# A selective scan after windowed attention on one core: TensorE's products dealt out anew over a chunk's slots, and one convolution tap moved to VectorE

## The reference, cut to what matters

```python
dt = softplus(einsum('nlr,dr->nld', dt, dt_proj_w) + dt_proj_b)
dA = exp(dt[..., None] * A)
dBx = dt[..., None] * Bm[:, :, None, :] * xc[..., None]
def step(h, inp):
    a, b, c = inp
    h = a * h + b
    return (h, jnp.sum(h * c[:, None, :], axis=-1))
```

## Time and profile before

| what | value |
|---|---|
| median of three runs | 10573.59 us (10556.45 to 10581.08) |
| the profiled execution's own time | 10566.67 us |
| its span in the trace | 10564.6 us |
| outside the span | 2.1 us |
| granted clock of PE, mean over the span | 0.899 |
| busy: PE, DVE, ACT, POOL | 8593.4, 8682.6, 6501.9, 6485.6 us |
| stage 1 ends, stage 2's first scan, its last scan ends | about 4.2 ms, 4228.1 us, 10266.8 us |

### The profile page before, as it was taken

One profiled execution on the slowest core, in us unless ns is written; L12 is line 12 of the kernel. 1 busy time (PEld: TensorE's weight loads), 2 busy tenths in 40 slices (PEclk: granted clock), 3 DMA queues, 4 the chain that ended last, 5 costly groups with the idle time before them and its releaser, 6 DMA issues. The chain is left out here.

```text
span 10564.6 us, 200712 instructions
## 1 busy us (share of the span) xinstructions
PE 8593.4 (81%) x61658; PEld 3655.3 (35%) x61658; DVE 8682.6 (82%) x10568; ACT 6501.9 (62%) x12597; POOL 6485.6 (61%) x4046
## 2 busy tenths in 40 slices
PE   6999999999899998877887877788887777787870
PEld 3555555555555554222222222222222222222220
DVE  6777777777777775999989999998989999998985
ACT  5666666666666665666656666665666666666653
POOL 3222222222222221888888898988888888888980
PEclk9999999999999998888888898988888889888885
DMA  2222322222322322111111111111111111111119
GB/s 68 69 69 70 77 71 69 69 69 71 80 74 73 75 74 52 33 41 33 37 37 33 36 39 33 41 33 33 40 35 33 41 33 36 39 33 35 40 40 277
DMA packets 855792, 591.01 MB, mean 56 GB/s; under 512 B 621424, under 2 KB 725872, under 8 KB 848464
## 3 DMA queue, kind: packets, MB, share of 16 engines
q1 hardware_dynamic: 751440, 423.61, 17.3%
q0 software_dynamic: 49152, 100.76, 2.6%
q10 hardware_dynamic: 54016, 51.91, 1.6%
HBM read 109.27 MB, written 103.81 MB: 20 GB/s over the span
## 5 line engine op out<-in xcount | busy, mean ns | idle before, releaser
L1217 POOL TENSOR_TENSOR b_hh<-b_hh,b_cn 128x1024 f32<-128x1024 f32 x1600 | 3833.7, 2414 | 496.0 <-DVE b_hh L1516 495.6
L1516 DVE TENSOR_TENSOR_SCAN b_hh<-b_dA,b_ub 128x512 f32<-128x512 f32 x2800 | 3369.6, 1206 | 0.0
L278 POOL DMA_DIRECT2D kvsel<-kv x1536 | 1103.1, 721 | 2885.3 <-issue 2455.3
L1357 ACT ACTIVATE b_dA<-b_db,b_negA 128x448 f32<-128x448 f32 x2800 | 1719.3, 633 | 1289.3 <-PE b_db L1609 1280.8
L1501 DVE TENSOR_TENSOR b_ub<-b_ub,b_bn 128x512 f32<-128x512 f32 x2800 | 1904.5, 680 | 543.2 <-PE b_ub L1609 528.0
L1609 PE MATMUL b_ub<-b_rows,b_pick 96*64 96x512 bf16 x6400 | 1407.6, 441 | 946.3 <-DVE b_hh L1516 901.3
L1609 PE MATMUL b_db<-b_rows,b_pick 96*64 96x512 bf16 x6400 | 1283.8, 424 | 203.5 <-ACT b_dA L1357 199.8
L1609 PEld LDWEIGHTS b_ub<-b_rows,b_pick 96*64 96x64 bf16 x6400 | 361.3, 110 | 3130.9 <-DVE b_hh L1516 2668.6
L554 DVE SCALAR_TENSOR_TENSOR oacc<-vpad,vec,oacc 128x1064 f32<-128x1064 f32 (+1 forms) x934 | 1199.7, 1302 | 11.4
L1645 PE MATMUL b_acc<-b_hh,b_gather 64*32 64x512 f32 x12800 | 1008.5, 692 | 3.0 <-POOL b_hh L1217 3.0
L395 ACT ACTIVATE prob<-score,nmax 128x256 f32<-128x256 f32 (+1 forms) x1600 | 735.9, 478 | 167.3 <-issue 96.1
(11 more groups left out here) (190 smaller groups left out, 13559.5 us busy)
## 6 DMA issues: line engine op xcount, KB each, us to landing
b_rows<-b_term SPq DMA_DIRECT2D x2400, 64.0 KB, 2.0
kvsel<-kv SPq DMA_DIRECT2D x1600, 64.0 KB, 2.1
kvsel<-kv POOLq DMA_DIRECT2D x1536, 64.0 KB
xpad<-in_x SPq DMA_DIRECT2D x18, 1568.0 KB, 10.7
ys<-ysb ACTq DMA_DIRECT2D x16, 1600.0 KB, 9.4
b_yc<-ys SPq DMA_DIRECT2D x100, 256.0 KB, 2.7
xr<-b_xo SPq DMA_DIRECT2D x100, 256.0 KB, 2.7
x<-x3pad SPq DMA_DIRECT2D x16, 1568.0 KB, 18.2
```

The costliest lines, as they stand in the source:

```text
L278: eng.dma_start(kvsel[:, slot, j, :, WPIX * t:WPIX * (t + 1)].unsqueeze(1), kv[:, bass.ds(at[t], 1), :, :]).then_inc((s_kv, s_kg)[j][slot] ...
L1217: nc.gpsimd.tensor_tensor(out=now, in0=now, in1=cn[:, par, :].unsqueeze(1).broadcast_to([C, 2, HT]), op=ALU.mult).then_inc(s_pm, 1)
L1357: nc.scalar.activation(later(dA[:, k % DEEP, :]), later(db[k % 2][:, :]), ACT.Exp, scale=negA[:, 8 * q + e:8 * q + e + 1]).then_inc(s_a, 1)
L1516: nc.vector.tensor_tensor_scan(hh[:, k // 2 % PDEEP, HT * (k % 2):HT * (k % 2 + 1)], rate, new, 0.0, ALU.mult, ALU.add).then_inc(s_sc, 1)
```

## The change

Three things are edited.

1. `PTAP` is 4: PE does four lepe taps and DVE 21, so `LEPES` is 63, and 38 instead of 35 of them are spread over the pairs.
2. PE's long products from slot 16 on stand elsewhere: `project_bc` in slots 17 and 21 (was 16 and 17), the second and third product of `conv_even` in slots 28 and 30 (was 26 and 28). Slots with repeats only are now 14, 16, 18, 20, 22, 26 and 29: no two of them are neighbours.
3. ACT's two `kept` follow: behind decay 24 and decay 28 (was 23 and 24).

```diff
-        PTAP = 5
+        PTAP = 4
...
                 decay(n, 23)
+                decay(n, 24)
                 if more:
                     kept(n + 1, nxt, 0)
-                decay(n, 24)
-                if more:
-                    kept(n + 1, nxt, 1)
                 decay(n, 25)
...
                 for k in range(28, 32):
                     decay(n, k)
+                    if k == 28 and more:
+                        kept(n + 1, nxt, 1)
...
-                    if s == 16 and more:
+                    if s == 17 and more:
...
-                    if s == 17 and more:
+                    if s == 21 and more:
                         project_bc(n + 1, nxt, 1, s_bn, ONE + 2 * n + 3)
...
-                    if s in (25, 26, 28) and before_end(n, 2):
-                        conv_even(n + 2, (25, 26, 28).index(s))
+                    if s in (25, 28, 30) and before_end(n, 2):
+                        conv_even(n + 2, (25, 28, 30).index(s))
```

## The result

The changed kernel takes 10401.73 us (median of four runs, 10394.62 to 10411.63), the kernel before beside it 10568.08 us. The ratio is 0.9843, 95% interval 0.9826 to 0.986: faster by 1.6%, about 166 us. The forecast of 10104 us promised 4.4%, and the range ended at 10270 us. The sign was right, the size was not.

What follows compares the result with a forecast made beforehand. Stage 2 was taken as bound by DVE's scans, lengthened by PE at low clock: 54.9 + 0.6 + 0.3 = 55.8 us a chunk against 60.4, so 460 us, plus 10 for the tap, giving 10104 us; range 10010 to 10270.

Steps and rivals of the forecast that it cites:

- What bounds the kernel: Stage 2: a chain through DVE's scans, lengthened by PE, late by 5.2 us a chunk where the clock is down.
- The fall behind slot 22 goes away: Units 20 to 31: project_bc in slot 21 keeps the clock up, worth 2.2 to 5.8 us a chunk.
- The rule that was weighed: TensorE clock: drops need long idle gaps, so order would not matter; the trace's fall followed pauses of about 1.1 us.
- POOL doesn't become the bound, but it has nothing left: Stage 2: POOL busy 53.6 us, under 54.9; slot 31's add waits for product 11, costing 0.6 us, bounds 0 and 1.2.
- Rival C: Chunk's end, slots 28 to 31: the fall moves there, all chunks take 65.5 us, 11074 us in all; chance 5%.
- Up to 4.8 us more where it ran over into the next chunk: Units 0 to 19: low clock carried over from slot 22's fall, 41.6 against 36.8 us, goes away too.
- The third term: Slots 6 and 8: the clock can still fall, 1.25 us in one chunk of four, so 0.3 us a chunk.
- The tap: Attention: moving one tap from PE to DVE gives -3.4 and +2.7 us an image, -10 us in all.
- No one engine is the bound: Attention, 107.2 us an image: PE busy 98.2, ACT 97.4, DVE 92.0, so the tap could give -110 to +62 us.
- The other signs: Profile after: clock 0.95 or more, L1501 idle about 90 us, units 20 to 31 in 18.1 to 19 us.
- Rival A: Slots 24 to 30 or behind 14 to 18: one fall left in every chunk, 57.1 us each, 10234 us; chance 15%.
- Rival B: Stage 2: the clock doesn't depend on the order, only slot 26's lost product helps, 10473 us; chance 6%.

Runs made afterwards that it cites:

- bc_alone: The kernel before with only project_bc in slots 17 and 21 and ACT's copies behind decays 24 and 28; 10483.8 us, ratio 0.9957.
- order_alone: The changed kernel with PTAP = 5 again, so only the long products and ACT's two copies move; 10440.54 us, ratio 0.9899.
- mid_early: The changed kernel with ACT's middle(0) of the next chunk moved in front of evac and decay 21; 10225.67 us, ratio 0.9697.
- tap_dropped: The kernel before with four taps on PE, the same twenty on DVE and tap 24 left out altogether; 10406.37 us, ratio 0.9871.
- tap_alone: The kernel before with PTAP = 4 and nothing else; 10441.34 us, ratio 0.9892.
- pool_less: The changed kernel with POOL's products of pairs 8 and 9 made for one unit instead of two; 10160.88 us, ratio 0.963.
- mid_on_before: The kernel before with only ACT's middle(0) moved before evac and decay 21; 10536.51 us, ratio 1.0002.

## Why the prediction was wrong, step by step

**What bounds the kernel: right.** The chain runs through DVE's scans, and PE's repeats and the clock lengthen it. **The fall behind slot 22 goes away: right,** in all chunks; the add of slot 23 takes 1.09 us, and bc_alone shows that the `project_bc` in slot 21 does it. **The rule that was weighed** was one of the Trainium skill ("TensorE: Matmul & The Clock Gate", section "Why this matters for your kernels"), which ties drops to long idle gaps; by it the order would not have mattered. The runs disagree: the kernel before, bc_alone and order_alone have the same work on PE and their falls at other places, and the fall in the timeline above followed pauses of 0.58 and 0.94 us. Only the falls at a loop's end have a long pause beside them (2 to 3 us), and in the changed kernel 18 of those 31 begin ahead of it.

**"POOL doesn't become the bound, but it has nothing left": this step failed.** It compared POOL's busy time, 53.6 us, with the chunk's 54.9, and priced the one wait it saw, at the add, at 0.6 us. What counts is where in the chunk POOL's idle time lies. Nearly all of it is in front of product 4 and of `last`; behind them stands an unbroken row of 22.8 us (6748.03 to 6770.81) that begins with a wait for ACT, and this row's end holds up scan 30 and the adds of slots 27 and 31. Measured, a chunk at full clock is 56.2 us instead of 55.5, small in itself. But with the pauses that it makes in PE the clock falls in 41 chunks more, and mid_early, which takes this wait away, gains 187 us of stage 2, 1.9 us a chunk (154 us by the ratios, 1.5 a chunk). The forecast had taken 0.6 for it, with 1.2 as the upper bound.

**Rival C's mechanism was real, in 41 of 98 chunks,** and had only 5% because it was priced as all or nothing. Its price was too high: the chunk of 59.0 us above lost 2.8 us against one at full clock, not 9.7, and the mean loss is 2.0. With that price the point from which it turns the sign would never be reached. A mechanism of this kind belongs into the forecast as a term, not aside as a rival.

**"Up to 4.8 us more where it ran over into the next chunk": this reading failed.** I took the 41.6 us of the third chunk for the effect of the fall at slot 22. It is the loop's end, which came with its own fall all 31 times, before as after. The clue was there: three cuts, and one of them a pass's last chunk. The loss was a part of the 60.4 us and no part of what the change mends, but the forecast took all of 60.4 - 54.9 for lateness that goes away. It had no term for the loop's end, and it costs 1.6 to 1.7 us a chunk. The third term, one fall in four chunks at scans 5 to 9 with 1.25 us each, came out right as a product: 37 of 98 chunks had one, with about 0.9 us each, so 0.3 us a chunk.

The sum, then: 55.8 us forecast, less the 0.6 that it held for POOL, plus 1.9 for POOL's row and the falls behind it and 1.6 for the loop's end, gives 58.7, where 59.2 was measured. The rest is what even mid_early's best chunks have over the floor of 54.9 (55.4 us in the mean of those without a fall). Of the 3.4 us that were missed, the loop's end is the largest part.

**The tap: the sign was right, the term mis-sized.** -10 us was -3.4 from PE and +2.7 from DVE an image. Measured, in the same units: PE 72 / 16 = -4.5, DVE +1.6, so -2.9 us an image. "No one engine is the bound" held. I halved PE's relief, and two thirds of it came through; and I charged DVE the difference between a pair with two taps and one with a single tap, though half of a tap goes into time in which DVE waited. What PE's relief does to DVE's wait for scores, and what the taps then take of it, stands in the pages of the kernel before, tap_dropped and tap_alone, in this order:

```profile
L525 DVE TENSOR_REDUCE nmax<-score 128x2 f32<-128x512 f32 (+1 forms) x800 | 513.9, 684 | 211.3 <-PE score L796 210.8
...
L525 DVE TENSOR_REDUCE nmax<-score 128x2 f32<-128x512 f32 (+1 forms) x800 | 513.1, 682 | 131.7 <-PE score L796 131.4
...
L525 DVE TENSOR_REDUCE nmax<-score 128x2 f32<-128x512 f32 (+1 forms) x800 | 513.3, 683 | 116.9 <-PE score L796 116.9
```

So 80 us of the wait went with PE's tap, and DVE's further taps lie in 15 us more of it and in 16 us of its wait for ACT before the reciprocal (L532, 111.2 to 95.6 us): 31 of their 62 us cost nothing.

The attention takes 103.8 us, 3.4 less than before; the list of signs had said within 3 us.

**The other signs.** Clock over stage 2: 0.94, where 0.95 or more was named. Idle time before L1501: 304.5 us, over the 250 from which I had said I would be wrong. POOL idle for over 3 us a chunk while DVE waits: no, POOL is idle for 5.6 us a chunk, but for 0.3 only while DVE is idle too. PE waits for POOL before an add: yes, 47.5 us. Units 20 to 31: 19.0 to 19.6 us instead of 18.1 to 19. These signs, taken together, point to the end of a chunk, which is where the loss was. Rival A (one fall is left, 10234 us) comes nearest in kind: a fall was left in three chunks of four, but at the end, not in slots 24 to 30. Rival B is refuted by bc_alone.

## What to carry to other kernels

Before a stall is priced out of a chunk, look for the next engine not by its busy share but by its longest row without a pause: what starts that row, and what hangs on its end. Cut chunks over a whole pass of a loop, its last one among them, and count a disturbance by position before calling it a mean. And where TensorE's clock falls beside small pauses, a wait that is mended in one place can bring new ones in another: the same move of one ACT operation was worth nothing before the change and 1.5% behind it.

## What was not expected of the hardware

- An end of the loop that goes back costs PE about 2 to 3 us without an instruction (1.7 to 3.4 us), and it came with a fall of the clock to 1.2 GHz every time (31 of 31 before, after and in mid_early); in pool_less, where nothing else was late, all 31 falls begin inside that pause. From 32 to 8 passes stage 2 went from 5727.1 to 5630.1 us, 4.0 us for each pass saved (5.0 by the ratios).
- Falls outside the loop's ends followed PE pauses of about 1 us (0.94 at slot 31 after, 1.09 at slot 22 before), while pauses of 0.57, 0.31 and 0.19 us at the end of mid_early's chunk left the clock at 1.00. But the length of one pause doesn't decide it. In the changed kernel 24 of 66 chunks away from the loop's ends have the same pause of 0.94 to 1.10 us at slot 31 and no fall, and in the kernel before all 66 have one of 0.95 to 1.27 us there and none falls; a fall at slot 22 lay behind three such pauses in four slots, 1.08, 1.09 and 1.09 us. What decides it is open.
- Stage 2 of tap_alone, the same program as before, took 5967.7 us, and that of tap_dropped 5975.1, where the kernel before and mid_on_before took 6038.7 and 6019.3. The falls at scans 21 to 23 are as many but shorter: 35 of 99 lasted over 13 us in the kernel before, 18 and 20 of 100 in the two others. The medians bear it out: tap_alone is 102 us under the kernel before beside it and tap_dropped 134, where stage 1 explains 46 and 72. With the new order this gain is gone: 5904.7 us without the tap edit and 5914.0 with it. Something in how chunks and the clock's changes fall together may differ between the two; what, no run here tells. If it is real, it is why the sum of the parts exceeds the whole.
- 23 to 56 falls at scans 5 to 9 are in all versions, next to slots 6 and 8, which have repeats alone. They weren't tried.
